# Exponentials taken clip by clip from the scores in PSUM, with the negated maximum as their bias, in an audio tower's attention

## What is computed

```
h = tokenizer(x)                      # windows of 8 frames, two relu layers, batch norm: (32, 93, 256)
h = h + attention(layernorm(h))       # 16 heads of 64
h = h + experts(layernorm(h))         # one shared expert and 2 of 8 routed ones

attention(x), for each head:
    scores = q k^T * scale            # scale = 1 / (64 * 64 * 16)
    attn = softmax(scores)            # over the 93 tokens of the clip
    out = attn v, all heads joined, times WO
```

## Time and profile before

| | |
|---|---|
| median of three runs | 1059.61 us (1059.19 to 1060.35) |
| the profiled execution's own time | 1057.71 us |
| its span, first to last instruction | 1056.1 us |
| busy: TensorE, its weight loads | 1022.4 us (97%), 951.6 us (90%) |
| busy: VectorE, ScalarE, GpSimd | 619.5 us (59%), 503.7 us (48%), 423.3 us (40%) |
| granted TensorE clock, mean | 0.999 |

### The profile page before, as it was taken

How to read it: one execution, slowest core, us unless ns; L and a number is a source line. 1 busy time by engine, 2 the same in 40 slices (tenths; PEclk the granted TensorE clock), 3 DMA queues, 4 the chain that set the end, 5 groups by cost and what they waited for, 6 DMA issues and landing times. The chain is left out here.

```text
span 1056.1 us, 24354 instructions
## 1 busy us (share of the span) xinstructions
PE 1022.4 (97%) x8436; PEld 951.6 (90%) x8437; DVE 619.5 (59%) x1608; ACT 503.7 (48%) x1127; POOL 423.3 (40%) x539
## 2 busy tenths in 40 slices
PE   7997999999999999999999899999999999999997
PEld 7996888888888888888888798999999999999997
DVE  5665666767777676877757664433334443363565
ACT  4543445444544545454444554545445554355342
POOL 1001562335353443525343340707760746301886
PEclk9999999999999999999999999999999999999999
DMA  9626999900010000001011344322334224111564
GB/s 182 129 60 229 358 345 344 320 17 15 31 28 29 24 34 15 15 29 29 29 24 38 103 152 138 112 89 88 94 127 139 95 91 137 45 60 44 162 167 123
DMA packets 104084, 113.22 MB, mean 107 GB/s; under 512 B 29824, under 2 KB 94816, under 8 KB 104032
## 3 DMA queue, kind: packets, MB, share of 16 engines
q1 hardware_dynamic: 75532, 73.72, 22.9%
q0 software_dynamic: 17632, 27.02, 8.7%
q10 hardware_dynamic: 10868, 11.80, 3.4%
HBM read 49.43 MB, written 62.95 MB: 106 GB/s over the span
## 5 line engine op out<-in xcount | busy, mean ns | idle before, releaser
L1373 POOL TENSOR_TENSOR prob<-prob,rc 93x372 f32<-93x372 f32 x128 | 102.8, 804 | 269.8 <-DVE rc L1239 269.4
L968 PE MATMUL pj_ps<-xg,wA 128*128 128x372 f32 x768 | 150.2, 341 | 4.7 <-DVE split L794 2.7
L968 PEld LDWEIGHTS pj_ps<-xg,wA 128*128 128x128 f32 x768 | 127.5, 188 | 12.6 <-DVE split L794 3.8
L1926 DVE TENSOR_TENSOR act_s<-sc_ps,act_s 128x384 fp32r<-128x384 f32 (+1 forms) x84 | 41.4, 494 | 160.6 <-ACT sc_ps L1774 159.3
L1772 ACT ACTIVATE act_s<-sc_ps 128x384 fp32r<-128x384 f32 (+1 forms) x84 | 36.9, 440 | 147.4 <-PE sc_ps L1669 144.2
L954 PE MATMUL pj_ps<-wB,xg 128*93 128x512 f32 x384 | 102.6, 403 | 0.8 <-ACT h_s L716 0.8
L1142 ACT ACTIVATE probT<-t_ps 93x372 f32<-93x372 f32 x128 | 60.6, 473 | 84.2 <-PE t_ps L989 83.8
L1565 POOL DMA_INDIRECT raw<-y_rows,y_at x48 | 63.2, 1316 | 79.1 <-issue 78.8
L1243 DVE TENSOR_TENSOR oT<-o_ps,oT 128x372 fp32r<-128x372 f32 x64 | 34.8, 544 | 89.6 <-ACT oT L1147 89.4
L1683 PE MATMUL dn_ps<-wA,act_s 128*128 128x256 f32 x720 | 85.1, 278 | 0.0
L1683 PEld LDWEIGHTS dn_ps<-wA,act_s 128*128 128x128 f32 x720 | 83.0, 188 | 0.0
(11 more groups left out here) (223 smaller groups left out, 2131.1 us busy)
## 6 DMA issues: line engine op xcount, KB each, us to landing
slots<-zeros SPq DMA_DIRECT2D x8, 3072.0 KB, 23.1
y_rows<-zeros SPq DMA_DIRECT2D x5, 2688.0 KB, 21.1
rows_in<-slots SPq DMA_DIRECT2D x22, 384.0 KB, 3.5
y_rows<-rows_out ACTq DMA_DIRECT2D x22, 384.0 KB, 2.6
raw<-in_L_ffn_routed_up POOLq DMA_DIRECT2D x7, 1024.0 KB, 5.4
raw<-in_L_ffn_routed_down POOLq DMA_DIRECT2D x7, 1024.0 KB, 8.1
ln_out<-split SPq DMA_DIRECT2D x8, 744.0 KB, 3.2
frames<-in_x SPq DMA_DIRECT2D x8, 400.0 KB
```

The source lines that it names most:

```text
L968: ins = pe.matmul(pj_ps[:, t, 0:N], wA[:, wp, at:at + P], xg[:, dp, m, :], start=(k == 0), stop=(k == 5))
L1373: pool.tensor_tensor(p, p, rc[:, u % 2, :].unsqueeze(2).broadcast_to([TP, 4, SL]), ALU.mult).then_inc(scaled, 1)
```

## The change

The subtraction is gone. VectorE's reduction writes the negated maximum of each clip. ScalarE evaluates exp(score - maximum) with four instructions a head, one for each clip, 93x93 each, which read the scores in their PSUM bank, take the negated maximum (one number a partition) as bias and write to `prob`. The scale is applied to q when ScalarE copies it out of PSUM. With that the waits change: scores(j) wait for the exponentials of pair j-1 (`exp_done`) where they waited for the subtractions (`shifted`), the exponentials wait for the maximum and for `prob`'s slot, and a maximum waits for the exponentials two heads back, which read the same slot of `mx`. `shift` is now called `maxima` and stands in the same places.

```diff
--- before.py
+++ after.py
@@ -604,7 +604,6 @@
             rw_lo = sem(c, "rw_lo")
             scores_done = sem(c, "scores_done")
             max_done = sem(c, "max_done")
-            shifted = sem(c, "shifted")
             exp_done = sem(c, "exp_done")
             sum_done = sem(c, "sum_done")
             recip_done = sem(c, "recip_done")
@@ -973,7 +972,7 @@
                 def scores(g, j):
                     for t in range(2):
                         pe.wait_ge(taken[t], number(g, "qk"[t] + str(j), back=0 if j else 1))
-                    ge(pe, shifted, g * NU + 2 * j)
+                    ge(pe, exp_done, g * NU + 2 * j)
                     for b in range(GB):
                         cols = slice(b * TP, (b + 1) * TP)
                         for h in range(2):
@@ -1094,7 +1093,7 @@
                     output(g, NJ - 1)
                     pe.wait_ge(sx_in, 16)
                     pe.wait_ge(sh_lo, SH_PARTS)
-                    pe.wait_ge(shifted, NG * NU)
+                    pe.wait_ge(exp_done, NG * NU)
                     for f in range(2):
                         shared_up(pe, sc_ps[:, f, 0:N], f)
 
@@ -1109,7 +1108,7 @@
 
                     take(g, "q%d" % j)
                     ge(act, scores_done, n * NJ + (j - 1))
-                    act.activation(qT[:, j % 2, :], pj_ps[:, 0, 0:N], ACT.Copy).then_inc(taken[0], 1)
+                    act.activation(qT[:, j % 2, :], pj_ps[:, 0, 0:N], ACT.Copy, scale=SCALE).then_inc(taken[0], 1)
 
                 def take_k(g, j, n):
 
@@ -1132,9 +1131,12 @@
                     ins.then_inc(affine, 1)
 
                 def exps(g, u):
-                    act.wait_ge(shifted, g * NU + (u + 1))
-                    act.activation(prob[:, u % 4, :, 0:SL], prob[:, u % 4, :, 0:SL], ACT.Exp, scale=SCALE
-                                   ).then_inc(exp_done, 1)
+                    ge(act, turned, g * NU + (u - 3))
+                    act.wait_ge(max_done, g * NU + (u + 1))
+                    for b in range(GB):
+                        ins = act.activation(prob[:, u % 4, b, 0:SL], s_ps[:, u % 2, b * TP:b * TP + SL], ACT.Exp,
+                                             bias=mx[:, u % 2, b:b + 1])
+                    ins.then_inc(exp_done, 1)
 
                 def take_turned(g, u):
                     act.wait_ge(turned, g * NU + (u + 1))
@@ -1222,14 +1224,12 @@
                         ins = dve.tensor_tensor(at, at, y_ps[0:R, i, 0:(hi - lo) * HD], ALU.add)
                     ins.then_inc(h_added, 1)
 
-                def shift(g, u):
+                def maxima(g, u):
+
                     dve.wait_ge(scores_done, g * NJ + (u // 2 + 1))
+                    ge(dve, exp_done, g * NU + (u - 1))
                     s4 = s_ps[:, u % 2, 0:4 * TP].rearrange("p (i t) -> p i t", i=4)[:, :, 0:SL]
-                    dve.tensor_reduce(mx[:, u % 2, :], s4, AX, ALU.max).then_inc(max_done, 1)
-                    ge(dve, turned, g * NU + (u - 3))
-                    dve.wait_ge(max_done, g * NU + (u + 1))
-                    dve.tensor_tensor(prob[:, u % 4, :, 0:SL], s4, mx[:, u % 2, :].unsqueeze(2).broadcast_to([TP, 4, SL]),
-                                      ALU.subtract).then_inc(shifted, 1)
+                    dve.tensor_reduce(mx[:, u % 2, :], s4, AX, ALU.max, negate=True).then_inc(max_done, 1)
 
                 def total(g, u):
                     dve.wait_ge(exp_done, g * NU + (u + 1))
@@ -1258,7 +1258,7 @@
                         if early:
                             total(g, s - 1)
                         if s % 2 == 0:
-                            shift(g, s)
+                            maxima(g, s)
                         if s == NU - 1 and behind and ahead:
                             take_ranks(dve, g, g - 1)
                         if behind:
@@ -1268,7 +1268,7 @@
                         elif behind and not early:
                             total(g - 1, NU - 1)
                         if s % 2 == 0:
-                            shift(g, s + 1)
+                            maxima(g, s + 1)
                         if behind:
                             routing(s, 1, g - 1, ahead)
                         if s == 13 and ahead:
```

## The result

The changed kernel takes 1189.3 us (median of four, 1187.3 to 1191.3) against 1060.0, a ratio of 1.121 (1.118 to 1.125). The profiled execution took 1191.3 us, 133.6 more than the one of before. The sign was forecast; the size, 1150 us in a range up to 1175, was not.

What follows compares the result with a forecast made beforehand. TensorE was taken to set the pace, at a fixed clock of 1.00. Stalls of 68 (six middle groups), 12.4 (first) and 10.3 (last), 91 us on 1057.7, give 1148.7; the median's 1.9 makes it 1150, range 1131 to 1175.

Steps and rivals of the forecast that it cites:

- The exponentials' price: ScalarE in attention: four small exponentials take 1.04 us, 0.54 more than the one now; bounds 0.78 and 1.34 us.
- plain: Stall of TensorE ahead of scores(j) at j = 2, 4, 6 of a middle group: 1.58 us each.
- j = 7: Last pair of a middle group: no v tile between two turns, so ScalarE comes late; scores 2.1 us later.
- j = 5: Middle group: scores 1.6 us later, less TensorE's 0.40 wait for the split, which goes: 1.2 us.
- The term of j = 1: Middle group, rows tile and its copy between: 1.8 us; first group's rows tile comes 0.54 us later.
- the rival on the clock: Granted clock falls to 1.2 GHz through a third of the attention stage, 80 us: 1230 us, chance 0.02.
- The range: Exponentials' bounds at 65 places, -17 or +20 us: 1133 to 1170; a tenth of a microsecond each widens to 1131 and 1175.
- Longer stalls: ScalarE falls behind at every pair, 2.1 us at 56 places plus 12, 130 us: 1195 us, chance 0.08.
- Shorter stalls: Four small exponentials take 0.6 us, 28 us less over 65 places: 1122 us, chance 0.06.
- faster: Bank free before TensorE needs it, shorter maximum-to-sum chain ends 12.2 us of idleness: 1048 us, chance 0.02.
- no effect: Bank free before TensorE comes to it, but nothing given back: 1060 us, chance 0.01.
- What costs nothing: Negated maximum, its wait, moved scale, wait for prob, and hidden sum, reciprocal and GpSimd scaling chains: no added time.

Runs made afterwards that it cites:

- The late wait alone: The kernel before with one edit, scores(j) wait for the exponentials of the pair before, not its subtractions: 1115.6 us.
- the early order: The changed kernel with both heads' exponentials in the even step for pairs 0 to 6: 1064.1 us; the kernel before with the same order: 1067.5 us.
- the biased four: The kernel before with scores waiting for the exponentials, done as four in-place instructions with a pointer bias of zeros: 1211.4 us.
- The fill of six matmuls: The changed kernel with six 512-column matmuls ahead of the scores' wait for the odd head's exponentials, pairs 1 to 7: 1146.8 us.
- the kernel with four exponentials: The kernel before with each exponential done in four in-place instructions of 93 columns, immediate scale, subtraction and waits kept: 1066.0 us.
- the kernel with two filling matmuls: The changed kernel with two filling matmuls ahead of the wait of the scores: 1151.7 us.

## Why the prediction was wrong

- **What bounds the kernel, and where the change makes TensorE wait: right.** 56 waits of the scores for the exponentials were forecast, at j = 1 to 7 in eight groups, and there are 56 at those places. (That the list has 56 under ScalarE's name too is chance: of the 59 in all it has three short ones at j = 0 among them and puts three of the others down to VectorE.) The late wait alone made the stall, the early order took it away.
- **The exponentials' price: right.** 1.04 us for four was forecast, 1.01 measured (one 0.339, start to start 0.22). The rule of the Trainium skill, "ScalarE: Activation LUTs", section "What ACT_TABLE_LOAD costs", gave 1.15 for the same, too much here; in SBUF, where the biased four took 1.15, it fits.
- **The sum of the stalls: right.** 91 us forecast, 87.2 us more idleness measured. Term by term: plain 1.55 (forecast 1.58), j = 7 1.98 (2.1), j = 5 1.53 less the absorbed 0.40 (1.2). The term of j = 1 was too small: its rows tile waits for the affine copies in seven groups (5.0 us in 7 times), and not in the first group alone, since these stand behind head 0's longer exponentials in every group but the last. In the middle group at 338.7 us the scores came 2.2 us late, not 1.8. That the total is still 4 us below the forecast is in part offset: the plain term and those of j = 5 (1.13 measured) and j = 7 were a little too large.
- **The step that failed: the rival on the clock.** The prediction took the granted clock of 1.00 as fixed in the sum, gave its fall a chance of 0.02, and argued that waits of 0.9 us stand in the stage at 1.00 and that no slice was lower. Those waits were few and at most 0.9 us long; the change made 56 of 1.5 to 2.0 us. A trace that has no such stall can't show what one does to the clock, so the row was no evidence against it. I also priced the rival at 80 us on top by a made-up share, a third of the stage at 1.2 GHz; it was 42.5 us, and a mean clock of 0.93 means about a seventh of the stage. What the runs showed in place of a fixed clock is a second term of 42.5 us that hangs on the stalls. The fill of six matmuls gave 1146.8 us, 3 us from the forecast of 1150: with the clock held, the sum was right to 0.3%.
- **The range.** Its last step doesn't follow from what is said: a tenth of a microsecond at 65 places is 6.5 us, which on 1133 and 1170 gives 1127 and 1177, not 1131 and 1175. The measured 1189.3 is outside either.
- **The rivals.** "Longer stalls" came out near the measured time (1195; its own 130 us on 1059.6 give 1190) for a reason that isn't there, so that is luck: the plain stalls were 1.55 us, not 2.1. "Shorter stalls", "faster" and "no effect" are out.
- **What costs nothing: right, all but a little.** In the same early order the changed kernel is 3 us faster than the one before, and it isn't faster in any order than the kernel before in its own. ScalarE's added time is not quite free where it stands (5 us of idleness in the kernel with four exponentials).

## What to carry to other kernels

When a buffer is handed back by a later reader, look for what stands ahead of that reader in its own queue: if it waits for the instruction that TensorE does just before it needs the buffer, the whole chain is a stall, whatever the averages say, and moving the reader ahead of that wait removes it. If TensorE has run without gaps so far, a forecast with new, repeated gaps as long as those here (means of 1.05 to 1.68 us, which cost 1 to 55 us in clock) needs a second term, the work that is then done at 1.2 GHz, and an upper end that holds it. For that term the longest gaps say more than the mean. Filling matmuls in a stall are a cheap way to tell the two terms apart, and where the stall can't be removed they give the second one back.

## What the runs showed of the hardware that was not expected

In the changed kernel the granted clock fell from 1.00 to 0.50 behind idle stretches of 1.56 to 2.01 us, some with a shorter one just ahead, with TensorE busy on both sides of them. Each of those 22 times it came back with TensorE busy throughout; in the drain it stayed down for 20 us with TensorE busy in 20.17 of 21.00, and why is open. These falls cost 42.5 us in one stage. In the kernel whose stalls were 1.07 us in the mean and 1.3 at most there was none in the stage. Shorter idle stretches brought a fall too where two stood close together (0.63 and 1.21 us in the kernel with two filling matmuls; 0.74 and 1.12 in the drain of the early order). An exponential of 93x93 took 339 ns from PSUM with a pointer bias, 363 ns from SBUF with one, and 271 ns from SBUF with an immediate scale.
